# Layer 1 of a two-layer convolution and attention kernel: block scores and selection placed inside the first head's token steps

## The reference

```
qkv = einsum('oc,bcl->bol', qkv_w, gn(x))            # q, k, v per head and token
qb, kb = mean over the 64 tokens of each block of q, k
_, lut = top_k(einsum('bhnd,bhmd->bhnm', qb, kb), 6) # for each query block 6 key blocks
o_s  = softmax(q . k of the 6 blocks) . v             # full attention inside the 6 blocks
c_q, c_k = softmax over the 64 features of q, k
kvb[m], ksum[m] = sum over the tokens of block m of c_k v, c_k
comp = 1 - one_hot(lut)                               # the 58 other blocks
o_l  = (c_q . sum_m comp kvb[m]) / (c_q . sum_m comp ksum[m] + eps), through proj_lw, proj_lb
out  = out_w . (o_s + o_l)
```

## Time and profile before

| | us |
|---|---|
| three timed runs: median (lowest to highest) | 9156.37 (9153.67 to 9159.21) |
| the profiled execution, its own time | 9132.41 |
| its span, first to last instruction of the program | 9130.6 |
| TensorE busy in it | 7661.6 (84%) |
| VectorE, GpSimd, ScalarE busy | 5047.8, 3797.0, 3522.8 |
| mean granted TensorE clock | 0.91 |

### The profile page before, as it was taken

The page is one execution under the profiler, slowest core; times in us unless marked ns, Lnnn a source line. Parts: engine busy times, 40 slices in busy tenths (PEclk is TensorE's granted clock), DMA queues, the critical chain, the costliest instruction groups (busy, mean ns, idle before and its releaser), DMA issues.

```text
span 9130.6 us, 206107 instructions
## 1 busy us (share of the span) xinstructions
PE 7661.6 (84%) x65004; PEld 5202.2 (57%) x65004; DVE 5047.8 (55%) x11563; ACT 3522.8 (39%) x9207; POOL 3797.0 (42%) x10084
## 2 busy tenths in 40 slices
PE   8978899788997879978899787997889978899778
PEld 5645566555565555555556555565555655555555
DVE  3475644756446564475644756447564465644656
ACT  1145621455214462144521455214452145521455
POOL 2335533355333553344533355334453344533444
PEclk9988899888998899988899889998899988999889
DMA  3201122011220112201122011220112201122111
GB/s 100 65 15 26 38 88 65 15 26 38 89 65 15 26 40 87 65 16 27 39 87 65 15 26 42 84 65 17 26 47 78 65 17 26 50 75 65 21 22 54
DMA packets 398743, 431.90 MB, mean 47 GB/s; under 512 B 159184, under 2 KB 355984, under 8 KB 393296
## 3 DMA queue, kind: packets, MB, share of 16 engines
q1 hardware_dynamic: 397648, 418.42, 16.2%
HBM read 102.76 MB, written 67.63 MB: 19 GB/s over the span
## 4 chain that ended last, share of the span: by engine, by line
PE 54%; DVE 23%; issue 7%; DMA 6%; ACT 5%; DVEq 3%; SPq 1%; POOL 1%; POOLq 0%; ACTq 0%
PE PS L621 12%; PE PS L684 7%; DVE arena L1132 5%; PE PS L902 5%; DVE arena L1222 4%; PE PS L771 4%; PE PS L867 3%; PE PS L664 3%; PE PS L827 3%; PE PS L836 3%; DVE SM L1346 3%; ACT arena L1076 2%; DVEq L1334 2%; PE PS L652 2%; DMA kv_rows<-arena 2%
## 5 line engine op out<-in xcount | busy, mean ns | idle before, releaser
L971 ACT ACTIVATE arena<-PS 128x128 f32<-128x128 f32 (+5 forms) x4160 | 1552.4, 399 | 2072.8 <-PE PS L621 598.2
L559 POOL COPY arena<-arena 64x129 f32 x6144 | 1537.7, 294 | 1386.7 <-PE PS L873 1136.1
L483 POOL TENSOR_TENSOR arena<-arena 128x512 f32<-128x512 f32 x768 | 806.4, 1072 | 1459.4 <-PE PS L621 1443.9
L621 PE MATMUL PS<-arena 128*128 128x256 f32 x6144 | 1360.3, 380 | 48.5 <-DMA arena<-arena 48.1
L1132 DVE COPY arena<-PS 64x260 f32<-64x260 f32 (+2 forms) x1272 | 634.4, 515 | 1362.4 <-PE PS L621 527.6
L621 PEld LDWEIGHTS PS<-arena 128*128 128x128 f32 x6144 | 1156.7, 189 | 272.9 <-issue 95.6
L1132 DVE COPY arena<-arena 64x129 f32 x4096 | 855.7, 271 | 414.5 <-PE PS L873 298.0
L807 PE MATMUL PS<-arena 64*64 64x192 f32 x8192 | 714.7, 391 | 249.5 <-POOL arena L559 227.6
L1222 DVE RECIPROCAL arena<-arena 128x512 f32<-128x512 f32 x256 | 857.6, 3350 | 119.0 <-ACT arena L1019 117.4
L489 POOL TENSOR_TENSOR BUF<-BUF,arena 128x512 f32<-128x512 f32 x256 | 358.5, 1400 | 1283.2 <-ACT arena L1007 1283.2
L1346 DVE TENSOR_REDUCE SM<-PS 128x1 f32<-128x384 f32 x1024 | 570.8, 557 | 540.2 <-issue 411.1
(11 more groups left out here) (102 smaller groups left out, 10581.1 us busy)
## 6 DMA issues: line engine op xcount, KB each, us to landing
arena<-arena SPq DMA_DIRECT2D x1024, 128.0 KB, 2.3
arena<-arena SPq DMA_DIRECT2D x768, 144.5 KB
BUF<-in_x SPq DMA_DIRECT2D x18, 2048.0 KB, 11.5
kv_rows<-arena SPq DMA_DIRECT2D x256, 130.0 KB, 3.5
arena<-kv_rows SPq DMA_DIRECT2D x256, 130.0 KB
out<-BUF SPq DMA_DIRECT2D x64, 512.0 KB, 2.6
arena<-in_taps SPq DMA_DIRECT2D x96, 288.0 KB, 3.7
W<-in_w SPq DMA_DIRECT2D x2, 768.0 KB, 5.6
```

The costliest lines, as they stand in the source:

```text
L483: last = pool.tensor_tensor(o, tap, mix, ALU.mult)
L559: last = pool.tensor_copy(G[p % GD][0:D, j // 3, j % 3, :], KVB[0:D, bass.ds(off, KVW)])
L621: last = nc.tensor.matmul(bank(i)[:, a * 256:(a + 1) * 256], lhsT=TW[n % 2][:, a * CH + k * P:a * CH + (k + 1) * P], rhs=src[:, k // 2:k / ...
L971: return nc.scalar.activation(o, i, ACT.Copy)
```

## The change

The pieces of work around the selection become small functions and are called from within head 0's token steps. In TensorE's program the matmuls of the block scores move from ahead of the token stage to behind the third step's q, k and v (p = 2). Token steps p = 0, 4, 8 and 12 of head 0 wait for the quarter of XN that they read; before, the wait for the block sums covered that. `turn(0)` waits for the copy of the scores, no longer for the offsets. In ScalarE's program the copies to QB and KB move behind the third step's copies. In VectorE's program the first reduction stays ahead of step 0; the second follows step 0, the copy of the scores step 1, maxima, places and offsets step 2, and the six rounds of the selection steps 3 to 8. A new semaphore tells TensorE that SEL is whole.

```diff
@@ TensorE
-                    pe.wait_ge(s_xbm, b + 1)
-                    for h in range(NH):
...
-                    last.then_inc(s_sc, 1)
+                    def block_scores():
+                        pe.wait_ge(s_xbm, b + 1)
...
+                        last.then_inc(s_qkb, 1)
+                        pe.wait_ge(s_qkc, b + 1)
+                        settle(pe)
...
+                        last.then_inc(s_sc, 1)
@@ turn(p)
                                 if p == 0:
-                                    pe.wait_ge(s_idx, b + 1)
+                                    pe.wait_ge(s_scc, b + 1)
@@ token steps of TensorE
+                                if h == 0 and p % 4 == 0:
+                                    pe.wait_ge(s_xna, b * 8 + 4 + p // 4 + 1)
+                                    pe.wait_ge(s_xnd, b * 8 + 4 + p // 4 + 1)
...
                                 last.then_inc(s_qp, 1)
+                                if h == 0 and p == 2:
+                                    block_scores()
                                 if p >= 2:
                                     turn(p - 2)
...
+                            if h == 0:
+                                pe.wait_ge(s_sel, b + 1)
@@ ScalarE
-                    act.wait_ge(s_qkb, b + 1)
-                    copy(QB[0:D, :], PS[0:D, 5, 0:4 * NBLK])
-                    copy(KB[0:D, :], PS[D:P, 5, 0:4 * NBLK]).then_inc(s_qkc, 1)
...
+                                if h == 0 and p == 2:
+                                    act.wait_ge(s_qkb, b + 1)
+                                    copy(QB[0:D, :], PS[0:D, 5, 0:4 * NBLK])
+                                    copy(KB[0:D, :], PS[D:P, 5, 0:4 * NBLK]).then_inc(s_qkc, 1)
@@ VectorE
+                    block_sums(0)
                     for hp in range(2):
...
                                 nc.vector.tensor_tensor(feat, qk, mx.unsqueeze(3).broadcast_to([P, 2, 2, D]),
                                                         ALU.subtract).then_inc(s_sub, 1)
+                                if h == 0 and p == 0:
+                                    block_sums(1)
+                                elif h == 0 and p == 1:
+                                    copy_scores()
+                                elif h == 0 and p == 2:
+                                    top_blocks()
+                                elif h == 0 and p < 3 + TOPK:
+                                    select(p - 3)
                                 if p >= 5 and p % 2:
                                     store_kv((p - 5) // 2)
```

More of the change, by code:

```diff
@@ L262, in build @@
         s_sc = sem("block_scores")
+        s_scc = sem("block_scores_copied")
+        s_sel = sem("selection_made")
         s_idx = sem("block_indices")
@@ L715, in _ @@
                         group_sum(b, 1, k)
-                    pe.wait_ge(s_xbm, b + 1)
-                    for h in range(NH):
[L719 to L728, removed]
-                    last.then_inc(s_sc, 1)
+                    def block_scores():
+                        pe.wait_ge(s_xbm, b + 1)
+                        for h in range(NH):
+                            for kt in range(KT):
+                                last = nc.tensor.matmul(PS[:, 5, h * NBLK:(h + 1) * NBLK], lhsT=W1[:, kt, h, 0:2 * D],
+                                                        rhs=XBM[:, kt, :], start=(kt == 0), stop=(kt == KT - 1))
+                        last.then_inc(s_qkb, 1)
+                        pe.wait_ge(s_qkc, b + 1)
+                        settle(pe)
+                        for h in range(NH):
+                            cols = slice(h * NBLK, (h + 1) * NBLK)
+                            last = nc.tensor.matmul(PS[0:D, 7, cols], lhsT=QB[0:D, cols], rhs=KB[0:D, cols],
+                                                    start=True, stop=True)
+                        last.then_inc(s_sc, 1)
                     pe.wait_ge(s_zero1, b + 1)
@@ L1253, in _ @@
                     scale(1)
[L1254 to L1279, removed]
+                    def block_sums(kt):
+                        if kt == 0:
+                            dve.wait_ge(s_xnd, b * 8 + 8)
+                            nc.vector.tensor_reduce(XBM[:, 0, :], XN[:, 0, :].rearrange("p (m t) -> p m t", m=NBLK), AX.X,
+                                                    ALU.add)
+                        else:
+                            dve.wait_ge(s_xna, b * 8 + 8)
+                            nc.vector.tensor_reduce(XBM[:, 1, :], XN[:, 1, :].rearrange("p (m t) -> p m t", m=NBLK), AX.X,
+                                                    ALU.add).then_inc(s_xbm, 1)
@@ new lines, in copy_scores, with top_blocks @@
+                    def copy_scores():
+                        dve.wait_ge(s_sc, b + 1)
+                        order.after(copy(SC[0:D, :], PS[0:D, 7, 0:4 * NBLK]))
+                        dve.sem_inc(s_scc, 1)
+                    def top_blocks():
+                        settle(dve)
+                        for head in range(NH):
+                            last = nc.vector.max(MX8[0:D, 8 * head:8 * head + 8], SC[0:D, head * NBLK:(head + 1) * NBLK])
+                        order.after(last)
+                        settle(dve)
+                        for head in range(NH):
+                            last = nc.vector.max_index(IU[:, 8 * head:8 * head + 8], MX8[0:D, 8 * head:8 * head + 8],
+                                                       SC[0:D, head * NBLK:(head + 1) * NBLK])
+                        order.after(last)
+                        upper = lambda tile: tile.rearrange("p (h k) -> p h k", h=NH)[:, :, 3:6]
+                        order.after(copy(IDXF, IU))
+                        order.after(nc.vector.tensor_scalar(upper(IU), upper(IU), 1, None, ALU.bitwise_xor))
+                        nc.vector.tensor_scalar(IDX, IU, float(KVW), None, ALU.mult).then_inc(s_idx, 1)
@@ L1280, in _, with select @@
+                    def select(k):
+                        for head in range(NH):
+                            picked, at = SEL[:, head * NBLK:(head + 1) * NBLK], IDXF[:, 8 * head + k:8 * head + k + 1]
                             if k == 0:
@@ L1285, in _ @@
                         order.after(last)
+                        if k == TOPK - 1:
+                            dve.sem_inc(s_sel, 1)
+                    block_sums(0)
                     for hp in range(2):
```

## The result

| | median, us | lowest to highest | runs |
|---|---|---|---|
| kernel before | 9156.37 | 9134.97 to 9164.35 | 5 |
| changed kernel | 9089.51 | 9057.69 to 9102.91 | 5 |

The ratio is 0.9923, 95% interval 0.9897 to 0.9948: 67 us less, and clear of no change. The forecast was 48 us less, 9108, with a range of 9078 to 9140.

A forecast was written before the change was run, and what follows sets the result against it. Up to step 3 the VectorE-TensorE chain bounds the kernel, from step 4 TensorE. Per image 9.4 - 2.4 - 1.0 = 6.0 us, for eight images 48 us: 9156.4 - 48 = 9108 us, range 9078 to 9140.

The forecast's parts named there:

- head start: Turn to layer 1, each image: step 3's maxima start at 535.8 where they started at 545.22, 9.4 us earlier.
- Step 0 ahead of the second reduction: VectorE, turn to layer 1: putting step 0 first makes the second reduction end 1.0 us later.
- the list: Signs expected in the changed profile, among them VectorE's wait for the scores at about 3.5 us, step 1 ahead of it.
- rival on the clock: TensorE's token steps: clock dips once in steps 4 to 9 (9132, chance 0.08) or stays low (9254, chance 0.06).
- the dip: TensorE, steps 4 to 9: about two steps run at 1.2 GHz, 3 of the 6 us go; 9132, chance 0.08.
- give-back: Steps 4 to 9: selection rounds make VectorE the bound, 14.6 us against 12.16, 2.4 us back; GpSimd takes 1.0 more.
- the 0.2 us a round for GpSimd: VectorE, steps 4 to 8: selects beside GpSimd's work take 0.2 us more a round, five rounds, 1.0 us.
- my second rival: Steps 4 to 8: each of twenty selects waits for a whole GpSimd copy, 6.4 us more; 9152, chance 0.12.
- The copies that I set against that rival: Trace of before: four VectorE copies beside six of GpSimd take 1.02 us against 0.64, only 0.38 us lost.
- the rounds hide entirely: Steps 4 to 8: rounds fit in time TensorE and ScalarE are ahead, cost nothing; 75 us less, 9081, chance 0.12.
- GpSimd blocks the selects: Steps 4 to 8: every select waits for a GpSimd copy, 0.6 us an image left; 9152, no change, chance 0.12.
- the two clock cases: TensorE: one dip in steps 4 to 9 (9132, chance 0.08), or low from step 5 to 15 (9254, chance 0.06).

The follow-up runs named there:

- e5: Changed kernel with the first reduction done twice, the second time into a spare place; ratio to the kernel before 0.9984.
- e2: Changed kernel with both reductions ahead of token step 0; ratio to the kernel before 0.9924.
- e4: Changed kernel again without an edit, second profile and more runs; median 9064.78 us, ratio to the kernel before 0.9939.
- e8: Kernel before again without an edit, for a second profile; ratio 0.9996.
- e1: Changed kernel with one round of four compares with the sixth largest score in place of six selection rounds; median 9039.40 us, ratio to the kernel before 0.991.
- e7: Changed kernel with four compares in place of the six rounds and both reductions ahead of step 0; ratio to the kernel before 0.9918.
- e3: Changed kernel with the six rounds in steps 3, 4, 6, 8, 10 and 12; median 9039.20 us, ratio to the kernel before 0.9919.

## Why the prediction was right

**The head start.** It said 9.4 us at step 3, with its maxima 21.3 us after the first reduction's start. Measured: 9.74 us, 20.96. The way there was as worked out: 5.80 us from the end of the second reduction to the copy of the scores (524.55 to 530.35) did not change, and e5 shows that what is put ahead of it is paid in full. Step 0 ahead of the second reduction cost 0.78 us (5.12 us between the two starts instead of 4.34) and not 1.0; e2 gave 0.75 of it back. I had VectorE wait about 3.5 us for the scores; it was 4.19. My own working, 5.80 less the 1.6 for `sums(0)` and step 1, gives 4.2, so that was a slip of the list, and the sum didn't use it. Step 4 followed step 3 by 2.66 us in the mean and not by 2.9, which adds 0.2 to the head start.

**The clock.** It was 0.50 during the block scores and up to about 536.1, some 5 us after TensorE resumed at 530.97; I had taken 5.8. From there it stayed 1.00, with TensorE busy 82% in steps 4 to 9. Neither rival on the clock came true in the changed kernel's steps 4 to 15; the dip shows in two images of e5.

**The give-back.** Forecast 2.4 us for the rounds and 1.0 for GpSimd, 3.4 in all. Measured: from step 4 to step 9 14.95 us against 12.17 in the mean, 2.78, and 0.33 more between step 9 and step 15: 3.1. The term that was mis-sized is the 0.2 us a round for GpSimd. A round took 0.93 to 0.95 us beside GpSimd against 0.89 alone, so 0.05 a round. What GpSimd takes, it takes from the subtraction: 0.81 us in steps 5 to 8, where I had 0.60, the middle of 0.42 and 0.78. Of the 1.0 us only 0.4 came in steps 4 to 8 (2.78 less 2.4). The 0.33 came in step 9, which my working held free: VectorE still ran without a wait there. That the total was only 0.3 off is in part luck, a term too large beside one left out.

The Trainium skill, "SBUF — State Buffer", section "Who interferes with whom", lets a VectorE instruction with two SBUF inputs and a GpSimd instruction that reads SBUF exclude each other, so that the second waits until the first has finished; my second rival took that for every select. The rows of the selects don't agree: a round of four takes 0.05 us more beside copies of some 0.3 us each, and the copies 0.71 us for two where the earlier trace rows have 0.64. The copies that I set against that rival in the prediction were the weaker evidence, as they read one input and a select reads two. For the subtraction the rows come near the rule: it starts 0.08 us into a multiplication of 0.61 us and takes 0.39 us longer than alone, where a wait until the end would add 0.53.

**The sum.** 9.92 us at step 4, less 2.78 and 0.33, is 6.81 us an image and 54.5 us, where I had 6.0 and 48. e4 repeats it with 60.29 - 53.66 = 6.63 against e8. The 56 us of the runs beside e4 agree with that number; the first 67 us have some 12 more, within the spread of their runs (9057.69 to 9102.91). Of the 18.5 us between my 9108 and the measured 9089.51, 6.5 are thus the larger head start (54.5 against 48), and 12 lie in stages for which I had put no change.

**The rivals.** That the rounds hide entirely is refuted by e1 (3.15 us to be had), that GpSimd blocks the selects by the rows above, and the two clock cases by the stretches at 1.00.

## What to carry to other kernels

A chain that runs through several engines in turn is the place to put independent steps, and what set the gain here was the order on the engine that holds the chain's long instructions: moving TensorE's work alone gave nothing. Work spread over later steps costs what the engine that does it has no room for; in each step look for its waits, count those as cover once only, and look at the step behind it too: a wait that is filled can leave the next step with an instruction that meets another engine's. Better than to hide work is to drop it: four compares with the sixth largest score do, but for equal scores, what twenty-four compares with indices did, and e1 and e7, 0.8 to 0.9% below the kernel before, have the shortest token stage of all kernels here; by time they can't be told from e3.

## What the runs showed of the hardware

Runs of one and the same kernel on one chip lie far apart beside a gain of this size: six of the changed kernel between 9025.19 and 9077.14 us, with a mean granted clock from 0.923 down to 0.915. Two of its profiles, one from each set of its runs, differ by 32.6 us in their spans; head 0's stretches up to step 15 agree within 0.1 us an image in the mean, so 32.0 us of that lie in the other stages. A gain of 0.1% is therefore read from the stretch of a profile where it arises and not from the median.
